# A fused attention and ternary-FFN block: part of each activation load moves from SyncE's queue to GpSimd's, w_gate and w_up are prepared ahead of w_down, and w_down's transpose gets one name

## What is computed

```python
x = x + layernorm(attn(layernorm(x)))        # x: (8, 4096, 1024) f32
x = x + layernorm(ffn(layernorm(x)))

def attn(x):
    xa = x @ (W_attn + lora)^T                       # 3072 channels
    xa = (xa - xa.mean((0, 1))) * rsqrt(xa.var((0, 1)) + EPS) * gamma + beta
    q, k, v = split(xa)
    y = softmax(causal(q @ k^T / sqrt(1024))) @ v
    return (y @ W_proj^T) @ (W_proj + lora)^T

def ffn(x):
    h = silu(bitlinear(x, w_gate)) * bitlinear(x, w_up)      # inner 4096
    return bitlinear(h, w_down)
# bitlinear: activations rounded to 8 bits by row, weights to -1, 0, 1
# times the mean of |w| over the whole matrix
```

## Time and profile before

| | |
|---|---|
| median of the runs | 6780.86 us |
| the runs | 6670.9 and 6890.83 us |
| the profiled execution | 6672.22 us |
| its span on the slowest core (core 1) | 6670.7 us |
| span of the eight cores | 6660.4 to 6670.7 us |
| PE, DVE, ACT, POOL busy | 63%, 40%, 13%, 12% |
| DMA queues | SP's 504.98 MB, POOL's 117.47 MB |

### The profile page before, as it was taken

One profiled execution on the slowest core, in us unless ns is written; L12 is line 12 of the kernel. 1 busy time (PEld: TensorE's weight loads), 2 busy tenths in 40 slices (PEclk: granted clock), 3 DMA queues, 4 the chain that ended last, 5 costly groups with the idle time before them and its releaser, 6 DMA issues.

```text
span 6670.7 us, 63898 instructions; the slowest of 8 cores (6660.4 to 6670.7 us)
## 1 busy us (share of the span) xinstructions
PE 4178.6 (63%) x19100; PEld 1775.2 (27%) x19100; DVE 2676.3 (40%) x3736; ACT 856.9 (13%) x1490; POOL 815.6 (12%) x2580
## 2 busy tenths in 40 slices
PE   5455555699899314555555562113777777757888
PEld 2111111222344112222222221002333333323444
DVE  2444444400444223333332323444555555555333
ACT  0222222100000000111111110112111111110000
POOL 0244444300000000000000000111000000000000
PEclk9988888899899657888888886555888888878999
DMA  3766666555022221000000003443111111123332
GB/s 126 229 193 191 188 193 189 174 176 177 31 86 83 91 60 44 33 32 24 24 24 24 24 15 126 150 152 92 38 38 38 38 38 44 42 85 117 114 114 98
DMA packets 240445, 626.53 MB, mean 94 GB/s; under 512 B 58680, under 2 KB 83304, under 8 KB 225704
## 3 DMA queue, kind: packets, MB, share of 16 engines
q1 hardware_dynamic: 207080, 504.98, 24.9%
q0 software_dynamic: 33024, 117.47, 4.7%
HBM read 450.39 MB, written 171.97 MB: 93 GB/s over the span
## 4 chain that ended last, share of the span: by engine, by line
PE 45%; DVE 20%; issue 12%; DMA 11%; POOL 9%; ACT 2%; DVEq 1%; POOLq 1%; SPq 0%; ACTq 0%
PE pall L1350 7%; PE pall L1234 5%; PE pall L680 5%; PE pall L1227 4%; PE pall L930 4%; PE pall L532 4%; DVE lnx L491 3%; PE pall L827 2%; DMA xt<-xnew_scr 2%; PE pall L845 2%; POOL lnx_scr L58 2%; POOL smalls L488 2%; PE pall L950 2%; PE pall L538 2%; PE pall L968 2%
## 5 line engine op out<-in xcount | busy, mean ns | idle before, releaser
L508 PE MATMUL pall<-lnx 128*128 128x512 bf16 x2048 | 612.3, 452 | 455.6 <-DVE lnx L491 455.6
L1234 PE MATMUL pall<-WuT,kqT 128*128 128x512 bf16 x2048 | 563.7, 425 | 146.2 <-DVE gu L1246 146.2
L1227 PE MATMUL pall<-WgT,kqT 128*128 128x512 bf16 x2048 | 523.7, 402 | 116.8 <-DVE smalls L1259 62.4
L1350 PE MATMUL pall<-WdT,gqT 128*128 128x512 bf16 x2048 | 468.0, 391 | 35.8 <-DVE gqT L1340 35.8
L508 PEld LDWEIGHTS pall<-lnx 128*128 128x128 bf16 x2048 | 204.5, 108 | 863.0 <-issue 729.4
L491 DVE TENSOR_SCALAR lnx<-xin,smalls 128x1024 bf16<-128x1024 f32 x256 | 208.0, 812 | 563.6 <-POOL smalls L488 563.6
L827 PE MATMUL pall<-Kfm,qfm 128*128 128x512 bf16 (+3 forms) x480 | 166.8, 527 | 371.8 <-DVE smalls L896 341.3
L473 ACT ACTIVATE dummy1k<-xin 128x1024 f32<-128x1024 f32 x256 | 270.9, 1058 | 737.3 <-DMA xin<-x_all 736.8
L680 PE MATMUL pall<-lnfm,WqkvT 128*128 128x512 bf16 x1536 | 346.3, 389 | 6.2 <-DVE lnfm L662 6.2
L1234 PEld LDWEIGHTS pall<-WuT,kqT 128*128 128x128 bf16 x2048 | 217.2, 107 | 455.1 <-issue 264.9
L930 PE MATMUL pall<-Vtm,S_f 128*128 128x512 bf16 x1056 | 253.7, 381 | 94.3 <-DVE S_f L923 94.3
(11 more groups left out here) (221 smaller groups left out, 4927.3 us busy)
## 6 DMA issues: line engine op xcount, KB each, us to landing
xin<-x_all SPq DMA_DIRECT2D x256, 512.0 KB, 4.1
lnx_scr<-lnx POOLq DMA_DIRECT2D x256, 256.0 KB, 4.3
lnb<-lnx_scr SPq DMA_DIRECT2D x256, 256.0 KB, 2.7
gq_scr<-gq SPq DMA_DIRECT2D x32, 1024.0 KB, 4.7
gq<-gq_scr SPq DMA_DIRECT2D x32, 1024.0 KB, 6.4
xa_scr<-stg SPq DMA_DIRECT2D x48, 512.0 KB, 2.9
XT<-x_all SPq DMA_DIRECT2D x32, 512.0 KB, 4.0
xnew_scr<-XT SPq DMA_DIRECT2D x32, 512.0 KB, 2.6
```

The costliest lines, as they stand in the source:

```text
L508: s.add("pe", (lambda q, p=p, i=i, h=h, bi=bi, t=t: q.matmul(bank(bi), lnx[:, p, i * 128:(i + 1) * 128], lnx[:, p, h * 512:(h + 1) * 512], ...
L1227: s.add("pe", (lambda q, blk=blk, cj=cj, gb=gb, p=p: q.matmul(bank(gb), kqT[:, p, cj, :], WgT[:, cj, blk * 512:(blk + 1) * 512], start=(cj ...
L1234: s.add("pe", (lambda q, blk=blk, cj=cj, ub=ub, p=p: q.matmul(bank(ub), kqT[:, p, cj, :], WuT[:, cj, blk * 512:(blk + 1) * 512], start=(cj ...
L1350: s.add("pe", (lambda q, ds=ds, ic=ic, p=p: q.matmul(bank(ds), gqT[:, p, ic, :], WdT[:, ic, ds * 512:(ds + 1) * 512], start=(ic == 0), sto ...
```

## The change

It has four parts. First, the load of an `xin` tile is split: SP loads columns 0 to 767 and a new DMA on POOL (`ldxh`) columns 768 to 1023, under two names that L471, L473 and L491 all read. Second, the load of an `lnb` tile is split in halves in the same way (`ldlbh` on POOL). Third, w_gate and w_up are prepared before w_down's scale. Fourth, WdT has one name in place of two. The lines of the changed kernel are 1 higher than before at L471 to L491, 10 higher at 1029 to 1098.

```diff
     def emit_ln(p, src_ap, src_res, dst_ap, dst_res):
+        srcs = [src_res] if isinstance(src_res, str) else list(src_res)
...
     def emit_ldx(t):
         p = t % 8
-        s.dma("sp", xin[:, p, :], x_all[t * 128:(t + 1) * 128, :],
-              writes=[f"R_xin{p}"], name=f"ldx{t}")
+        s.dma("sp", xin[:, p, 0:768], x_all[t * 128:(t + 1) * 128, 0:768],
+              writes=[f"R_xin{p}lo"], name=f"ldx{t}")
+        s.dma("pool", xin[:, p, 768:1024],
+              x_all[t * 128:(t + 1) * 128, 768:1024],
+              writes=[f"R_xin{p}hi"], name=f"ldxh{t}")
...
-        emit_ln(p, xin[:, p, :], f"R_xin{p}", lnx[:, p, :], f"lnx{p}")
+        emit_ln(p, xin[:, p, :], [f"R_xin{p}lo", f"R_xin{p}hi"],
+                lnx[:, p, :], f"lnx{p}")
...
-        s.dma("sp", lnb[:, p, :], lnx_scr[t * 128:(t + 1) * 128, :],
-              reads=[f"lnxs.{t}"], writes=[f"lnb{p}"], name=f"ldlb{t}")
+        s.dma("sp", lnb[:, p, 0:512],
+              lnx_scr[t * 128:(t + 1) * 128, 0:512],
+              reads=[f"lnxs.{t}"], writes=[f"lnb{p}lo"], name=f"ldlb{t}")
+        s.dma("pool", lnb[:, p, 512:1024],
+              lnx_scr[t * 128:(t + 1) * 128, 512:1024],
+              reads=[f"lnxs.{t}"], writes=[f"lnb{p}hi"], name=f"ldlbh{t}")
...
+    ffn_w_prep_1024(0, w_gate, WgT, "WgT", "g")
+    ffn_w_prep_1024(1, w_up, WuT, "WuT", "u")
+
     for dc in range(8):
         s.dma("sp", gu[:, 0:2048], w_down[dc * 128:(dc + 1) * 128, 0:2048],
               writes=["gu_lo"], name=f"mwd{dc}")
...
-    ffn_w_prep_1024(0, w_gate, WgT, "WgT", "g")
-    ffn_w_prep_1024(1, w_up, WuT, "WuT", "u")
...
-                reads=[PB[tb]], writes=["WdTlo" if dc < 4 else "WdThi"],
-                name=f"td5{dc}_{g4}")
+                reads=[PB[tb]], writes=["WdT"], name=f"td5{dc}_{g4}")
...
-                    reads=[f"gqT{p}", "WdTlo" if ds == 0 else "WdThi"],
-                    writes=[PB[ds]], name=f"dn{t}_{ds}_{ic}")
+                    reads=[f"gqT{p}", "WdT"], writes=[PB[ds]],
+                    name=f"dn{t}_{ds}_{ic}")
```

More of the change, by code:

```diff
@@ L470, in emit_ln @@
     def emit_ln(p, src_ap, src_res, dst_ap, dst_res):
+        srcs = [src_res] if isinstance(src_res, str) else list(src_res)
         s.add("dve", (lambda q: q.tensor_reduce(st_s[p], src_ap, AX.X, ALU.add)),
-              reads=[src_res], writes=[f"ls{p}"], name="red")
+              reads=srcs, writes=[f"ls{p}"], name="red")
         s.add("act", (lambda q: q.activation(
             dummy1k, src_ap, AF.Square, accum_out=st_q[p])),
-            reads=[src_res], writes=["dummy1k"], accum=[f"lq{p}"], name="sq")
+            reads=srcs, writes=["dummy1k"], accum=[f"lq{p}"], name="sq")
         s.add("pool", (lambda q: q.tensor_scalar(
@@ L492, in emit_ln @@
             dst_ap, src_ap, st_m[p], st_r[p], ALU.subtract, ALU.mult)),
-            reads=[src_res, f"lm{p}", f"lr{p}"], writes=[dst_res], name="nrm")
+            reads=srcs + [f"lm{p}", f"lr{p}"], writes=[dst_res], name="nrm")
     def emit_ldx(t):
         p = t % 8
-        s.dma("sp", xin[:, p, :], x_all[t * 128:(t + 1) * 128, :],
-              writes=[f"R_xin{p}"], name=f"ldx{t}")
+        s.dma("sp", xin[:, p, 0:768], x_all[t * 128:(t + 1) * 128, 0:768],
[3 more added lines that the diff above has]
+              writes=[f"R_xin{p}hi"], name=f"ldxh{t}")
     for t in range(8):
@@ L535, in _build @@
                 start=(t == 0), stop=(t == NT - 1))),
-                reads=[f"lnb{p}"], writes=[PB[i]], name=f"gB{t}_{i}")
+                reads=[f"lnb{p}lo", f"lnb{p}hi"], writes=[PB[i]],
+                name=f"gB{t}_{i}")
         for h in range(2):
@@ L541, in _build @@
                 start=(t == 0), stop=(t == NT - 1))),
-                reads=[f"lnb{p}", "ones_bf"], writes=[PB[4 + h]],
+                reads=[f"lnb{p}lo", f"lnb{p}hi", "ones_bf"], writes=[PB[4 + h]],
                 name=f"gU{t}_{h}")
```

## The result

The changed kernel is slower: 1.0199 times the time of the kernel before, 95% interval 1.0140 to 1.0257. Its profiled execution took 6807.05 us against 6672.22 us before, so +134.8; the forecast was 6791, or +119, in a range of 6770 to 6900. The direction and the range held, the sum was 16 us short, and the interval lies across the 2% line.

A forecast was written before the change was run, and what follows sets the result against it. Stage A was taken as bound by a DVE-POOL-DVE hand-over loop of 4.11 us a tile, stage B by PE. +121.5 (xin load) + 1 (lnb) - 3.5 (weight order) + 0 (WdT) = +119 on 6672.2 gave 6791 us, range 6770 to 6900.

The forecast's parts named there:

- Stage A, the term that decides: Input layernorm and half the Gram matrix: POOL's new load lengthens the hand-over loop by 0.49 us, 248 times, +121.5 us.
- The choice of 0.59 for the load: POOL's new xin load priced at 0.59 us, the first of a back-to-back pair, giving 0.49 us a tile.
- the lower reading, the bare duration: POOL's new xin load priced at its bare 0.54 us: 0.44 us a tile, +109 us.
- The first load: Start of the input layernorm: POOL's first eight loads take 4.7 us, done before the first reduce; cost 0.
- Stage B: PE-bound stretch after the input layernorm: POOL's lnb halves hidden except at the start, about +1 us once.
- The order of the weights: FFN weight preparation: w_gate and w_up before w_down saves 1.6 and 1.9 us, new joints cost nothing more; -3.5 us.
- both waits that the term took away: Weight preparation: an earlier first read, -1.6 us, and no wait of w_gate's first read behind w_down's mean, -1.9 us.
- The name of WdT: First down matmul: with one name, the wait for all of WdT is already met; 0 us.
- That the wait isn't hidden: Rival, POOL's new xin load: its wait or tail adds time, +231 in place of +121.5, 6901 us; chance 0.17.
- Tile 0's 0.51 us: Input layernorm's first tile: 0.51 in place of 0.15 us between statistics after a DMA; would alone make 6880 us.
- That stage B becomes bound by small packets: Rival, lnb loads: 1 KB pieces cost what 2 KB ones do, +46 us, 6837 us; chance 0.08.
- That POOL's load doesn't hold up the statistics: Rival, input layernorm: POOL hands over the load and goes on, not slower, 6670 us; chance 0.07.

The follow-up runs named there:

- pipe_pool: Kernel before, with the sums and statistics of tile t+1 put ahead of the normalising and store of tile t: 6396.3 us, ratio 0.9614.
- xin_late: Changed kernel, with POOL's load for tile t+7 issued behind the power instruction of tile t instead of behind the store: 6680.5 us, ratio 1.0030.
- xin_two: Changed kernel, with POOL's quarter of each xin load issued as two DMAs of 128 columns each: 6947.8 us, ratio 1.0425.
- pipe_sp: Kernel before, reordered as in pipe_pool, and with the store of lnx issued by SP in place of POOL: 6248.0 us, ratio 0.9401.
- order_only: Kernel before, with w_gate and w_up prepared ahead of w_down and nothing else: 6675.2 us, ratio 1.0008.
- xin_both_sp: Changed kernel, with both pieces of each split xin load issued by SP: 6675.3 us, ratio 1.0014.
- no_xin: Changed kernel, with xin loaded whole by SP again: total not used (lower clock on some cores); slowest core left alone 6670.9 to 6673.5 us.

## Why the prediction was right, and where it was off

*Stage A, the term that decides: the mechanism held.* Forecast 0.49 us a tile, measured 4.58 - 4.11 = 0.475; forecast period 4.60, wait of DVE "about 685" (688.5), stage "about 1182" (1184.4). The choice of 0.59 for the load was wrong, and the lower reading, the bare duration, nearer: the load takes 0.55, behind the store as in a pair, and 0.55 + 0.02 ahead of L477, less the 0.13 of before, is 0.44. L477 and its hand-over add 0.02 and the stretch up to the store another 0.02, which the sum didn't have. So 0.49 was right to 0.015 partly by two small errors that cancel.

*What 248 x 0.475 = 118 leaves out.* The stage grew by 125. I read the distances of all 256 normalisings in each kernel's trace. Before, two are 6.4 us and the median is 4.11; after, four are 6.9 and one 6.4, at a median of 4.58. In each of them POOL stands still ahead of a DMA; one of the pauses of the kernel after:

```profile
491.99 0.62 POOL L58 DMA_DIRECT2D lnx_scr<-lnx  x1 [1.48 <-DVE lnx L492]
494.89 0.55 POOL L58 DMA_DIRECT2D xin<-x_all  x1 [2.28 <-issue]
```

"issue" is time in which the engine waits for nothing that the profile shows. Counted in POOL's DMAs from the first one of stage A, the pauses stand at the 114th and 212th before (and in *pipe_pool*), at the 114th, 212th, 310th, 408th and 506th after and in *xin_late*, and in *xin_two* at seven places from the 114th to the 702nd. On every core they are exactly 98 DMAs apart, whether POOL issues one, two or three a tile. They go with the number of POOL's DMAs, not with tiles, time or the other instructions: *pipe_sp*, where POOL issues none in the stage, has no pause, and in the kernel after they go on in stage B, at the 604th and 702nd, where PE's work hides them. So the load brings three more pauses in stage A, 3 x 2.3 = 7 us, and 118 + 7 = 125 closes the sum. In *xin_late* four of the five fall where POOL waits anyway and cost 1.3 us each in place of 2.3; 4 x 1.3 + 2.3 against 2 x 2.3 is its +3 us. The two of before were in its trace, and 248/98 x 2.3 = 6 could have been forecast. What POOL does in them no run shows.

*The first load: cost 0 was wrong, it is +3.3.* The step counted issues (4.7 us of them before the first reduce) and not landings. In the kernel after the first reduce waits for its input for longer:

```profile
238.21 4.51 SPq L58 DMA_DIRECT2D xin<-x_all  x8
238.77 4.52 POOL L58 DMA_DIRECT2D xin<-x_all  x8 [235.35 <-POOLq L64]
247.24 1.22 DVE L472 TENSOR_REDUCE smalls<-xin 128x1 f32<-128x1024 f32 x1 [9.23 <-DMA xin<-x_all]
```

On this core it starts 9.0 us after SP's first issue; before it was 243.4 - 238.3 = 5.1. The mean of the eight cores is 7.6 (5.9 to 9.6) for 4.4 (3.6 to 5.2), so +3.2. This distance is the one to read, since the moment of SP's first issue itself moves by some us between executions: *order_only*, with the same code up to there, has its first reduce at 244.7 in the mean. In *xin_both_sp* the distance is 3.4 to 5.2, in *xin_late*, whose first eight are issued by POOL too, 6.1 to 9.0. So it hangs on POOL's share, once; whether on the first use of its queue or on pieces of eight tiles landing together, no run says.

*Stage B: +1 forecast, +0.2 measured.* POOL's halves lie beside PE's work, as the step said. Half-size pieces cost nothing: DMA share 0.59 at 172 GB/s where it had been 0.56 at 170.

*The order of the weights: -3.5 was wrong, it is zero.* *order_only* against the kernel before, in means of the eight cores: both waits that the term took away did shrink. The first read comes 4.3 us after POOL's first issue for 5.0, so -0.7 where -1.6 was forecast: the first pieces of w_gate take longer than the 3.3 that its median piece takes. From the start of w_down's last sum to DVE's next work on a tile it is 5.2 for 7.2, so -2.0 where -1.9 was forecast. The step that failed is the rest, which the term put at nothing. The second passes take longer, w_gate's by 0.7 and w_up's by 1.4, and so do the sums of w_down, by 1.5 (64.8 for 63.4), while w_up's sums take 0.4 less. On the core shown above the conversion of w_up's last tile waits 2.0 us for its load, which now goes out next to w_down's first pieces of 1 MB; on the one of before it doesn't wait. Why w_gate's pass and w_down's sums grow, no run says. In the same stretch the kernel after shows +4.6, *xin_late* +3.0, *xin_both_sp* +1.1 and *no_xin* +0.9, all with this order, and single cores of one execution differ by 9, so I don't explain the 4.6.

*The name of WdT:* from the first to the last down matmul 595.5 us in the mean before, 596.7 after, and single cores lie between 593 and 599 in both. Nothing that stands clear of this, as forecast.

*The rivals.* That the wait isn't hidden (6901) fell in the timeline, and by *xin_two*: two loads with two waits in 1.06 us. Tile 0's 0.51 us doesn't come back in the middle of the stage. That stage B becomes bound by small packets (6837) fell with its unchanged length. That POOL's load doesn't hold up the statistics (6670) fell with L477, which waits in line behind it 0.6 us after its reduce has ended.

*The sum.* Forecast +121.5 + 1 - 3.5 = +119. Measured +134.8 on the slowest core, which is +129.6 in the mean of the cores and 5.2 from their wider spread. Against the forecast the mean has 3.4 more in stage A, 3.3 at the start and 8.1 at the weights, 0.8 less in stage B, and 3.4 less in all other stretches. So the total came as near as it did partly because the end of the program, which nobody priced, gave 4.0 us back.

## What to carry to other kernels

A DMA issue on an engine that also computes is an instruction in its program: ask where in the loop it stands, and against what slack. Between a store and the statistics that the loop waits for it costs its whole length less the slack; where the engine waits anyway it cost 3 us in 1060, and on SP 1. When every engine is half idle and one wait (DVE for L488, 563.6 us) spans the stage, look for what can be started a tile earlier before anything is moved between queues: that gave 4 to 6% here, and the split could have given nothing.

## What the hardware showed that I had not expected

POOL is held up while DVE normalises. In *xin_late* its DMA, issued at 500.73, takes 1.08 us in place of 0.55 and ends at 501.81; the normalising ran from 500.88 to 501.69. In *pipe_pool* the store issued at 501.44 takes 1.05 in place of 0.63 and ends at 502.49; the normalising ran from 501.56 to 502.37. That store is the one of the tile before, so it needs nothing from this normalising. Each time the DMA was issued first, 0.11 to 0.15 us ahead, and ended 0.12 behind the normalising; the two traces have 238 such loads and 247 such stores. In *pipe_sp* the tiny L479 takes 0.62 in place of 0.19 and ends at 501.63, where the normalising ends at 501.58. Beside the reduce, which is longer, the statistics keep their 0.19, and in *xin_late* the store its 0.55 (502.26 to 502.81, the reduce from 501.61 to 502.82). The Trainium skill (SBUF — State Buffer, "SBUF: two separate sides") says that GpSimd shares a port pair with VectorE, that some of VectorE's operations hold it for a whole instruction, and that a DMA issued from GpSimd then waits too. The trace agrees in its form, that POOL gets on some 0.05 to 0.12 us after the end of the normalising. That it is this lock, no run isolates.

One core's DMA engines moved 320 GB/s through stage A of *pipe_sp*, with all eight cores at work, at a share of 1.00; the 191 of before had been no limit. And there is the pause of 2.3 us at every 98th DMA of POOL's, described above. The medians on which I built the forecast can't show it; the longest value of a wait hints at it (4.5 us in the earlier trace rows, where a usual one is 2.2).
